# A graph kernel for 128 graphs: the row of attention scores s2 spread by a transfer through memory in place of transposes on TensorE

## What is computed

```python
A = (adj != 0)
for i in range(3):                     # layer 0, on h = relu(layernorm(x))
    m = h @ weight[i]
    aggr = einsum('bst,bsd->btd', A, m)
    h = gru_cell(aggr, h)              # three gates of 256, from aggr and from h
x = x + h
h = relu(layernorm(x))                 # layer 1, attention
Wh = h @ W.T
s1, s2 = Wh @ a1, Wh @ a2              # one number per node each
e = leaky_relu(s1[:, :, None] + s2[:, None, :], 0.2)
att = softmax(where(adj == 0, -inf, e))
x = x + att @ Wh
```

## Time and profile before

| | us |
|---|---|
| median of 3 runs | 1818.8 (1817.42 to 1821.85) |
| the profiled execution | 1817.42 |
| its span, first to last instruction | 1815.6 |
| mean granted TensorE clock, share of full | 0.992 |

### The profile page before, as it was taken

How to read it: one execution, slowest core, us unless ns; L and a number is a source line. 1 busy time by engine, 2 the same in 40 slices (tenths; PEclk the granted TensorE clock), 3 DMA queues, 4 the chain that set the end, 5 groups by cost and what they waited for, 6 DMA issues and landing times.

```text
span 1815.6 us, 32208 instructions
## 1 busy us (share of the span) xinstructions
PE 1779.8 (98%) x10500; PEld 945.4 (52%) x10500; DVE 1419.7 (78%) x2827; ACT 1022.8 (56%) x1824; POOL 350.3 (19%) x758
## 2 busy tenths in 40 slices
PE   6999999999999999999999999999999999999995
PEld 5445555545555454555545555454554545555453
DVE  6667878787887878878787887878878777887877
ACT  5556555555556556555565556556555565556553
POOL 1012130311303113031221303113031221303100
PEclk8999999999999999999999999999999999999997
DMA  3322322332314223232322324223232332323121
GB/s 105 76 65 65 70 75 55 85 73 60 96 35 110 52 64 93 66 79 52 87 69 64 81 51 110 52 64 92 51 92 53 78 77 64 75 58 92 32 57 53
DMA packets 323712, 128.38 MB, mean 71 GB/s; under 512 B 239200, under 2 KB 323680, under 8 KB 323680
## 3 DMA queue, kind: packets, MB, share of 16 engines
q1 hardware_dynamic: 323680, 127.97, 29.9%
HBM read 52.96 MB, written 16.78 MB: 38 GB/s over the span
## 4 chain that ended last, share of the span: by engine, by line
PE 96%; issue 1%; DVE 1%; POOLq 0%; POOL 0%; DVEq 0%
PE r_bank L330 27%; PE z_bank L330 27%; PE hn_bank L330 14%; PE in_bank L330 14%; PE s_bank L330 3%; PE w_bank L330 3%; PE nb_bank L345 2%; PE nb_bank L344 2%; PE t_bank L799 1%; PE t_bank L810 1%; DVE dot_terms L1155 0%; DVE x_out L1111 0%; DVE tail_max L1186 0%; PE t_bank L330 0%; DVE u_lo L1201 0%
## 5 line engine op out<-in xcount | busy, mean ns | idle before, releaser
L903 ACT ACTIVATE n_out<-n_pre,bih 128x512 f32<-128x512 f32 x192 | 138.0, 719 | 238.9 <-DVE n_pre L1008 238.6
L330 PE MATMUL hn_bank<-ht_s,wh_hi 128*128 128x512 f16 x768 | 228.4, 379 | 1.7 <-PEq L438 1.7
L912 ACT ACTIVATE ht_s<-ht 128x512 f16<-128x512 f32 x128 | 80.6, 630 | 264.4 <-DVE ht L1024 264.4
L330 PE MATMUL r_bank<-ht_s,wh_hi 128*128 128x512 f16 x768 | 228.5, 379 | 0.0
L330 PE MATMUL z_bank<-ht_s,wh_hi 128*128 128x512 f16 x768 | 228.4, 379 | 0.0
L363 DVE TENSOR_TENSOR nb_lo<-nb_bank,nb_hi 128x512 f16<-128x512 f32 x192 | 131.0, 682 | 84.2 <-ACT nb_hi L359 84.1
L1003 DVE SCALAR_TENSOR_TENSOR n_pre<-tanh_r,hn_b 128x512 f32<-128x512 f32 x192 | 146.3, 762 | 62.2 <-ACT tanh_r L898 57.3
L307 POOL TENSOR_TENSOR ln_gnn<-stats_gnn 128x4 f32<-128x4 f32 x32 | 18.7, 583 | 893.6 <-DVE stats_gnn L260 893.6
L898 ACT ACTIVATE tanh_r<-r_bank,b_rz,down 128x512 f32<-128x512 f32 x192 | 147.2, 767 | 65.8 <-PE r_bank L330 65.7
L893 ACT ACTIVATE hn_b<-hn_bank,b_hn,down 128x512 f32<-128x512 f32 x192 | 147.9, 770 | 57.0 <-PE hn_bank L330 57.0
L907 ACT ACTIVATE tanh_z<-z_bank,b_rz,down 128x512 f32<-128x512 f32 x192 | 146.8, 764 | 26.3 <-PE z_bank L330 26.3
(11 more groups left out here) (248 smaller groups left out, 3938.3 us busy)
## 6 DMA issues: line engine op xcount, KB each, us to landing
x_in<-in_x_dram SPq DMA_DIRECT2D x32, 512.0 KB, 3.9
x_res<-in_x_dram SPq DMA_DIRECT2D x32, 512.0 KB, 4.1
out_dram<-x_out SPq DMA_DIRECT2D x30, 512.0 KB, 5.3
adj_in<-in_adj_dram SPq DMA_DIRECT2D x32, 256.0 KB, 4.0
adj_att<-in_adj_dram SPq DMA_DIRECT2D x32, 256.0 KB, 4.5
h_s<-ht_s SPq DMA_TRANSPOSE x128, 3.0
ht_s<-h_s SPq DMA_TRANSPOSE x64, 3.2
out_dram<-x_out SPq DMA_DIRECT2D x4, 256.0 KB, 2.2
```

What stands on the lines that cost most here:

```text
L330: last = nc.tensor.matmul(bank_ap, w, d, start=start and i == 0, stop=stop and i == len(todo) - 1)
L903: nc.scalar.activation(n_out[c][:], n_pre[c][:], ACT.Tanh, bias=bih[:, 4 + c:5 + c]).then_inc(n_ready, 1)
L912: nc.scalar.activation(ht_s[layer % 2][a][:, c, 0, :], ht[a][:, c, :], ACT.Copy, scale=HSCALE).then_inc(ht_hi_ready, 1)
```

## The change

SP stores s2 to memory (`store_s2`), 128 by 4 numbers, waits until this has landed, and loads it back onto all 128 partitions as one row of 512 numbers (`load_s2`, tile `s2_row`, graph index innermost). ACT adds s1 to this row as a bias, one activation for each graph (`scores` on ACT). DVE's addition L1071 and PE's four transposes a group are gone, with the waits around them. The tile `s12` becomes two tiles, `s1` and `s2`. The tail is as before but for these names.

```diff
@@ SIDE @@
-    (2, 5): [("neighbours", 1, 1, 1, 0)],
+    (2, 5): [("neighbours", 1, 1, 1, 0), ("store_s2", 1, -1)],
...
     (1, 6): [("scores", 0, -1)],
     (3, 6): [("scores", 1, -1)],
     (4, 1): [("softmax", 1, -1)],
+    (1, 1): [("store_s2", 0, -1)],
+    (1, 3): [("load_s2", 0, -1)],
+    (2, 7): [("load_s2", 1, -1)],
@@ tiles @@
-        s12 = both("s12", [P, GROUP, 2], F32)
+        s1 = both("s1", [P, GROUP], F32)
+        s2 = both("s2", [P, GROUP], F32)
+        s2_row = sb("s2_row", [P, P, GROUP], F32)
+        s2_dram = [nc.dram_tensor(f"s2_dram{a}", [P, GROUP], F32, kind="Internal").ap() for a in range(2)]
@@ SP @@
+                def store_s2(p, a):
+                    sp.wait_ge(dots_ready, per_group(p, a))
+                    sp.dma_start(s2_dram[a], s2[a][:]).then_inc(s2_stored[a], 16)
+
+                def load_s2(p, a):
+                    sp.wait_ge(s2_stored[a], per_load(p))
+                    wait_reached(sp, sum_ready, per_group(p, a) - 1)
+                    sp.dma_start(s2_row[:].rearrange("q t b -> q (t b)"),
+                                 s2_dram[a].rearrange("t b -> (t b)").unsqueeze(0).broadcast_to(
+                                     [P, T])).then_inc(s2_landed[a], 16)
@@ PE @@
-                    if a == 0 and c == 0:
-                        wait_reached(pe, sum_ready, per_group(p - 1, 1))
...
-                def scores(p, a):
-                    pe.wait_ge(dots_ready, per_group(p, a))
-                    if a == 1:
-                        pe.wait_ge(sum_ready, per_group(p, 0))
-                    else:
-                        pe.wait_ge(x1_ready, per_chunk(p, 1, 1))
-                    for b in range(GROUP):
-                        last = nc.tensor.transpose(t_bank[:, b * P:(b + 1) * P],
-                                                   s12[a][:, b, 1:2].broadcast_to([P, P]), ident[:])
-                    last.then_inc(s2_done, 1)
@@ ACT @@
+                def scores(p, a):
+                    act.wait_ge(s2_landed[a], per_load(p))
+                    wait_reached(act, minus_max_ready, per_group(p, a) - 1)
+                    for b in range(GROUP):
+                        last = nc.scalar.activation(score[:, b, :], s2_row[:, :, b], ACT.Identity,
+                                                    bias=s1[a][:, b:b + 1])
+                    last.then_inc(sum_ready, 1)
@@ DVE, scores @@
-                    dve.wait_ge(s2_done, n)
-                    wait_reached(dve, prob_ready, n - 1)
-                    nc.vector.tensor_tensor(score[:], t_bank[:].rearrange("p (b t) -> p b t", b=GROUP),
-                                            s12[a][:, :, 0:1].broadcast_to([P, GROUP, P]),
-                                            ALU.add).then_inc(sum_ready, 1)
                     dve.wait_ge(sum_ready, n)
```

More of the change, by code:

```diff
@@ L669, in graph_blocks @@
         res_t_done = sem("res_t_done")
-        gather_done, s2_done, attend_done = sem("gather_done"), sem("s2_done"), sem("attend_done")
+        gather_done, attend_done = sem("gather_done"), sem("attend_done")
         pt_landed = [sem(f"pt_landed{a}") for a in range(2)]
+        s2_stored = [sem(f"s2_stored{a}") for a in range(2)]
+        s2_landed = [sem(f"s2_landed{a}") for a in range(2)]
         hn_ready, tanh_r_ready, n_ready, tanh_z_ready = (sem("hn_ready"), sem("tanh_r_ready"), sem("n_ready"),
@@ L749, in _ @@
                     "tail_store": tail_store,
-                    "probs_transpose": probs_transpose,
+                    "probs_transpose": probs_transpose, "store_s2": store_s2, "load_s2": load_s2,
                     "transpose": transpose, "first_transpose": lambda *which: first_transpose_sp(sp, *which)})
@@ L849, in tail_row @@
                         last = nc.tensor.transpose(tail_row_banks[a][:, b * P:(b + 1) * P],
-                                                   s12[a][:, b, 1:2].broadcast_to([P, P]), ident[:])
+                                                   s2[a][:, b:b + 1].broadcast_to([P, P]), ident[:])
                     last.then_inc(tail_row_done, 1)
@@ L882, in _ @@
                     "residual": residual, "neighbours": lambda *which: neighbours_pe(pe, *which), "gather": gather,
-                    "scores": scores, "attend": attend, "tail_row": tail_row, "tail_probs": tail_probs,
+                    "attend": attend, "tail_row": tail_row, "tail_probs": tail_probs,
                     "tail_gather": tail_gather, "tail_attend": tail_attend})
@@ L991, in _ @@
                     "gather": gather, "softmax": softmax,
-                    "split_probs": split_probs, "tail_gather": tail_gather, "tail_apply": tail_apply,
+                    "split_probs": split_probs, "scores": scores, "tail_gather": tail_gather, "tail_apply": tail_apply,
                     "tail_u_hi": tail_u_hi, "tail_softmax": tail_softmax, "tail_pt_hi": tail_pt_hi})
@@ L1058, in dots @@
                                                                   c12[:, i, :], 1.0, 0.0, ALU.mult, ALU.add,
-                                                                  s12[a][:, b, i:i + 1])
+                                                                  (s1, s2)[i][a][:, b:b + 1])
                     if half == 1:
@@ L1174, in tail_scores @@
                     dve.wait_ge(tail_dots_ready, n)
-                    nc.vector.tensor_tensor(mask, mask, s12[a][:, graphs, 0:1].broadcast_to([P, 2, P]),
+                    nc.vector.tensor_tensor(mask, mask, s1[a][:, graphs].unsqueeze(2).broadcast_to([P, 2, P]),
                                             ALU.add).then_inc(tail_masked_ready, 1)
```

## The result

| | before | with the change |
|---|---|---|
| median, us (7 runs of each) | 1818.1 (1817.35 to 1821.85) | 1824.57 (1822.93 to 1827.08) |
| the profiled execution | 1817.42 | 1825.77 |
| its span | 1815.6 | 1823.8 |
| mean granted TensorE clock, share of full | 0.992 | 0.994 |

The ratio is 1.0035, with a 95% interval from 1.0024 to 1.0046. The forecast was 1803, and 1824.6 is outside its range. It went the way of rival C, which had a chance of 0.09.

The account below looks back on a forecast made before the run. Two loops bound the kernel: PE's, 109.18 us a pair, and a longer elementwise one, 109.39. PE's removed work, 13.2 us, plus its vanished waits, 2.5, made 15.7 us off, giving 1803, range 1799 to 1812.

Parts of the forecast that it names:

- rival C: Group 0's row round trip at (1, 6) bounds the pair; slower, at worst 21 us, 1840; chance 0.09.
- So the row lands at about 392.1: Group 0's row, loaded behind x_in and adj_in, lands at 392.1; ACT needs it at 392.58 for no delay.
- I take 2.5: Group 0's 2 KB store lands 2.5 us after issue, at 388.6; the range considered was 2.5 to 5.3.
- the bounds of 391.6 to 395.4: Row landing: 391.6 if a transfer's tail overlaps; 395.4 if the store took 5.3 and the load 4.0.
- g: Us a pair by which the elementwise loop shortens; gain is the smaller of 15.7 and 15 x g.
- PE's floor: PE's own loop without the transposes, 0.88 us less a pair: 108.30 us, below which nothing more is gained.
- 13.2 + 2.5 = 15.7: Total gain in us: 13.2 from PE's removed transposes over 15 pairs, 2.5 from PE's late starts in slot 3.
- Two loops: PE's loop, 109.18 us a pair, and an elementwise one through DVE, ACT and POOL, 109.39, run side by side; the longer paces.
- A change that took work only from PE would then gain nothing: With the elementwise loop longer, removing PE work alone gains zero; both loops have to get shorter.
- In slots 1 to 3 DVE is nearly without a gap: A DVE instruction there is on the elementwise loop, so removing L1071 saves 0.71 us twice a pair, 1.43.
- ACT's addition: One 128-column activation with bias takes 0.39 us, four 1.29, hidden in ACT's idle time; upper end 0.72 for one.
- The forecast thus has some 0.8 us of room: At (1, 6) the row may land some 0.8 us later than 392.1, including 0.34 forgiven by the loops' difference.

Follow-up runs that it names:

- e5_store_only: Changed kernel with both stores but no loads of the row in the loop; one row is loaded from input x ahead of the loop; 1801.43 us, ratio 0.9905.
- e6_load_only: Changed kernel without the stores; the row is the same 2 KB of input x, broadcast to all partitions at the same places; 1801.93 us, ratio 0.9907.
- e10_store_big: Changed kernel with stores but no row loads in the loop, each store writing 512 bytes from each partition in place of 16; 1800.27 us.
- e3_pe_only: Kernel before without PE's transposes of s2 in the loop and the waits around them; DVE's addition, ACT and transfers kept; 1814.48 us, ratio 0.9976.
- e1_swap: Changed kernel with group 0's row load moved right behind its store at (1, 1), ahead of the two input loads; 1810.87 us, ratio 0.9957.
- e2_early: Changed kernel with group 0's store and row load both moved to (0, 7), right behind the dots; 1802.51 us, ratio 0.9911.
- e11: Changed kernel with stores but no row loads in the loop, each store's 16-byte pieces going to an on-chip tile in place of memory; 1801.99 us.
- e8_contiguous: Changed kernel with group 0's store and load at (0, 7), and ACT reading 128 neighbouring floats in place of every fourth; 1801.72 us, ratio 0.9906.
- e9_store_early: Changed kernel with only group 0's store moved to (0, 7); the row's load stays at (1, 3) behind both input loads; 1801.60 us, ratio 0.9909.
- e4_dve_only: Kernel before with PE's transposes kept, but one DVE scaling in place of addition and leaky relu in each group's scores; 1814.53 us, ratio 0.9981.

## Why the prediction was wrong

**The step that failed** is the last one on the transfers: "So the row lands at about 392.1", 6.0 us after the store's issue. It was 397.03 - 388.72 = 8.3. Of its parts, "I take 2.5" for the store was too high, it took 1.9; the 3.5 from the load's issue to its landing was 6.4. I had reckoned the load's time from the bandwidth of the earlier trace rows, as if the transfers ahead ran as before. But the new store changes them: x_in went from 3.9 to 6.2. The store alone makes 5.3 of it (e5_store_only), the load alone 4.1 (e6_load_only), both together 6.2. Stretches of 1 us show where (last three columns: clock, DMA share, GB/s). First the second and the third microsecond after x_in's issue, with the change and then in e10_store_big, whose store has large pieces; then one that answers to the earlier trace rows:

```profile
390.46:391.46 1.00, 1.00 (x9) 0.53 (x8) 0.62 (x1) 1.00 (x3) 0.00 (x0) 1.00 0.22 13
391.46:392.46 1.00, 1.00 (x12) 0.65 (x10) 0.93 (x3) 0.59 (x1) 0.00 (x0) 1.00 0.78 173
```

```profile
385.01:386.01 1.00, 1.00 (x10) 0.54 (x8) 0.62 (x1) 1.00 (x3) 0.00 (x0) 1.00 0.77 160
386.01:387.01 1.00, 1.00 (x11) 0.60 (x9) 0.93 (x3) 0.59 (x1) 0.00 (x0) 1.00 1.02 346
```

```profile
394.00:395.00 1.00, 1.00 (x7) 0.44 (x5) 0.97 (x2) 0.81 (x2) 0.00 (x0) 1.00 0.76 258
```

So most is lost where x_in starts: 13 and 173 GB/s, where large pieces ahead leave 160 and 346 (small pieces without the row's load, e5_store_only: 63 and 172). That is about 0.3 MB fewer in two microseconds, some 1 us at 306 GB/s. The tail is slower as well, 258 where the sum had 306. The whole schedule is later here by 2.73 (the transposing DMA ahead starts at 387.32, at 384.59 in the earlier trace rows), so on the forecast's clock the row landed at 394.3. That is inside the bounds of 391.6 to 395.4, but the time's own range left that end out.

**The lateness adds up.** On the forecast's clock the row is 394.3 - 392.1 = 2.2 late (the store went out 0.1 sooner than assumed). Less the 0.48 of room before DVE feels it, plus 0.48 for ACT's longer additions, is 2.2; DVE shows 2.28 in the third pair. Over 14 pairs DVE waited 27.3 / 14 = 1.95 us, so with the 0.08 that such a wait hides about 2.03 a pair. Then g = 1.43 - 2.03 = -0.60, and the pair 109.39 + 0.60 = 109.99. Measured 109.86. The 0.13 between them is as much as POOL's stage gave back (see e3_pe_only): 109.39 was the length with POOL as it ran before. That this is the reason is a reading, not tried by a run. The same correction makes e1_swap's sum 108.93 where 109.01 was measured, so it does not close every sum. The rule gain = 15 x g gives 9 us slower, 7 with the correction; from the first to the fifteenth mask of group 0 the changed kernel's trace is 7.05 longer (1538.55 against 1531.50), and the medians say 6.5. Rival C was right in mechanism and sign (the row's round trip at (1, 6) bounds the pair), not in what would be long in it: it blamed the store's own landing. The Trainium skill's sentence on a "surprisingly long delay" of the final write (DMA: Bandwidth & Descriptors, Anatomy of one DMA) was cited for that; here it was 1.9 us in most pairs, 3.6 at most, 1.4 when issued at (0, 7), so the trace doesn't bear it out. (The section describes transfers issued from GpSimd; these are SP's.)

**What held.**
- PE's floor: 108.30 a pair forecast, 108.27 measured in all eight versions in which no row is late after the first pair (e2_early and e5 to e11; five of them leave s2 out of the scores and e8_contiguous puts it at the wrong places); a time of 1803 forecast, 1800.3 to 1802.5 measured there. "13.2 + 2.5 = 15.7" was 16.2 in the spans (1815.6 - 1799.4, e9_store_early).
- Two loops, and the elementwise one the longer: e4_dve_only and e1_swap came out within 0.05 a pair. The chain that ended last is no help in the kernel before: it gives PE 96% there, as in e9_store_early, where PE does set the pace. Only PE's late starts, 0.21 a pair, showed the other loop. Where that loop is longer by more, the chain does turn: PE has 14% of it in the changed kernel and 8% in e3_pe_only.
- At (3, 6) DVE gained its 0.71, with no wait for ACT.

**What was off.**
- "A change that took work only from PE would then gain nothing" was too strong: 0.25 a pair came off in e3_pe_only. The elementwise loop isn't independent of PE's times.
- "In slots 1 to 3 DVE is nearly without a gap" is not what the trace before shows: between 383 and 435 DVE idles ten times for 0.7 to 1.5 us. Seven of these are its 0.70 wait for ACT's high part of the state, which is elementwise work too, and e4_dve_only bore the conclusion out all the same.
- ACT's addition was 0.51 to 0.52, not 0.39. I had named this and taken the lower end. By itself it costs nothing: in e9_store_early the additions run from 389.57 and DVE doesn't wait.
- "The forecast thus has some 0.8 us of room" was a small margin to set against a transfer with no row behind it. A chance of 0.09 for all that a new kind of transfer can do to its neighbours was too low.

One thing is left unexplained: in the eleventh to fourteenth pair the store of group 0 took 3.0 to 3.6 us in place of 1.9, and the row behind it then landed in 4.4 to 4.8, not in 5.9 to 6.6. The two together changed little (ACT still waited 1.99 in the fourteenth). No run was made on it.

## What to carry to other kernels

The store in very small pieces cost next to nothing by its own landing here and 1 to 2 us by what it did to the transfers behind it: put it, and the round trip it begins, as early as its data allow and not directly ahead of loads that someone waits for. An engine with a busy share of 98% need not set the pace: look for late starts that recur once a period, follow them back until the path closes, and take the length of each loop before you price an edit on either. Where a forecast's room is smaller than the spread of its one term without a row, the sign is not settled.

## What the runs showed of the hardware that I had not expected

- 128 pieces of 16 bytes written to memory delay 512 KB of reads issued 0.8 us later by 1.1 us (mean of x_in 5.1 with the store alone, 4.0 in the kernel before), and by more when the row's load follows too. With pieces of 512 bytes, 32 times the bytes, there is no delay, and none with a tile on the chip as target.
- The same store landed in 1.4 us at (0, 7) and 1.9 behind a transposing DMA at (1, 1).
- ACT reads every fourth float at 0.52 us for 128 elements, neighbours at 0.39.
- A POOL instruction on 128 by 4 numbers takes 0.20 us, or 0.53 to 0.70, in the same place of the program; in the two traces shown the slow one is the one beside which a DVE instruction runs, and it ends 0.05 us behind it.
